# Layer norm tiles shared between VectorE and ScalarE, gate powers on GpSimd, residual and stores in pieces, and a new instruction order, in a small Flamingo decoder on one core

## The reference

```
for layer in 0..3:
    x = x + tanh(g_xattn[layer]) * attention_layer(layernorm(x), ctx)     # stages 0, 2, 4, 6
    x = x + tanh(g_ffn[layer])   * ffn_layer(layernorm(x))                # stages 1, 3, 5, 7
layernorm(x) = (x - mean(x)) / sqrt(var(x) + 1e-5)        # over the 128 columns
```

## Time and profile before

| | us |
|---|---|
| Median of 3 runs (316.25 to 316.88) | 316.64 |
| Profiled execution | 317.1 |
| Its span, first to last instruction | 315.3 |
| PE busy in the span | 296.9 |
| DVE busy | 231.4 |
| ACT busy | 149.2 |
| POOL busy | 63.7 |

### The profile page before, as it was taken

One profiled execution on the slowest core, in us unless ns is written; L12 is line 12 of the kernel. 1 busy time (PEld: TensorE's weight loads), 2 busy tenths in 40 slices (PEclk: granted clock), 3 DMA queues, 4 the chain that ended last, 5 costly groups with the idle time before them and its releaser, 6 DMA issues.

```text
span 315.3 us, 5757 instructions
## 1 busy us (share of the span) xinstructions
PE 296.9 (94%) x2088; PEld 199.5 (63%) x2088; DVE 231.4 (73%) x670; ACT 149.2 (47%) x330; POOL 63.7 (20%) x95
## 2 busy tenths in 40 slices
PE   8899999998899999999999999999999997998963
PEld 3463453793436488888888365589788774666431
DVE  4882985789768389796796495465558569999995
ACT  0448255422555864542306637523426538876411
POOL 5242454334100001000303301010311502211020
PEclk9999999999999999999999999999999999999999
DMA  6970300002200000000000000000000000000002
GB/s 185 309 248 0 102 13 3 0 2 75 73 0 2 0 2 0 3 0 2 0 0 2 3 1 2 0 2 0 0 2 0 2 1 0 3 0 0 3 0 67
DMA packets 8976, 8.73 MB, mean 28 GB/s; under 512 B 3547, under 2 KB 6901, under 8 KB 8949
## 3 DMA queue, kind: packets, MB, share of 16 engines
q1 hardware_dynamic: 8949, 8.37, 8.7%
HBM read 7.84 MB, written 0.52 MB: 27 GB/s over the span
## 4 chain that ended last, share of the span: by engine, by line
PE 65%; DVE 21%; ACT 6%; issue 3%; POOL 2%; DMA 2%; DVEq 0%; SPq 0%; ACTq 0%
PE psum L996 59%; DVE wide L1901 3%; DVE mx L1734 3%; ACT wide L1396 3%; PE psum L1090 2%; DMA early<-in_ffn 2%; DVE xn_t L1919 1%; DVE xn L1921 1%; DVE q L1914 1%; DVE wide L1908 1%; DVE wide L1907 1%; PE psum L1128 1%; DVE nmax L1868 1%; PE psum L1176 1%; PE psum L1184 1%
## 5 line engine op out<-in xcount | busy, mean ns | idle before, releaser
L934 POOL TENSOR_TENSOR nw<-mv,minus_half 128x2 f32<-128x2 f32 x32 | 22.2, 708 | 143.5 <-DVE mv L1597 143.5
L1396 ACT ACTIVATE wide<-psum 128x512 f32<-128x512 f32 x72 | 37.0, 607 | 14.9 <-PE psum L996 14.7
L1734 DVE TENSOR_REDUCE mx<-psum 128x4 f32<-128x308 f32 x96 | 38.6, 471 | 6.0 <-PE psum L996 5.9
L1396 ACT ACTIVATE q<-psum 128x512 f32<-128x512 f32 (+1 forms) x30 | 17.8, 597 | 36.0 <-PE psum L996 28.1
L996 PE MATMUL psum<-q_hi,first_hi 128*128 128x512 f32 (+1 forms) x68 | 30.6, 450 | 0.0
L996 PE MATMUL psum<-wide 78*128 78x386 f32 (+1 forms) x69 | 25.5, 507 | 3.0 <-DVE wide L1885 1.9
L996 PE MATMUL psum<-q_lo,first_hi 128*128 128x512 f32 (+1 forms) x68 | 26.8, 394 | 0.0
L996 PE MATMUL psum<-q_hi,first_lo 128*128 128x512 f32 (+1 forms) x68 | 26.7, 393 | 0.0
L996 PEld LDWEIGHTS psum<-early,wide 128*128 128x128 f32 x192 | 24.7, 191 | 2.3 <-ACT wide L1396 0.5
L996 PE MATMUL psum<-halves 128*128 128x512 bf16 x102 | 25.8, 379 | 0.0
L996 PE MATMUL psum<-early,wide 128*128 128x128 f32 x192 | 25.4, 276 | 0.1
(11 more groups left out here) (230 smaller groups left out, 562.8 us busy)
## 6 DMA issues: line engine op xcount, KB each, us to landing
early<-in_ffn SPq DMA_DIRECT2D x8, 256.0 KB, 4.8
w_attn<-in_attn SPq DMA_DIRECT2D x1, 640.0 KB, 7.4
w_attn<-in_attn SPq DMA_DIRECT2D x2, 288.0 KB, 6.4
x<-in_x SPq DMA_DIRECT2D x2, 256.0 KB, 3.6
w_ffn<-in_ffn SPq DMA_DIRECT2D x1, 512.0 KB, 7.2
early<-in_ffn SPq DMA_DIRECT2D x1, 512.0 KB, 3.7
out<-x SPq DMA_DIRECT2D x2, 256.0 KB, 2.3
rows<-in_rows SPq DMA_DIRECT2D x1, 468.0 KB, 6.1
```

Source lines behind the costliest of these rows:

```text
L934: G.tensor_tensor(nw[:, b, 2, tiles], mv[:, b, tiles, 1], minus_half[:, tiles], ALU.pow)\
L1396: A.activation(dst, banks.bank(*name)[0:rows_, 0:cols_], fn, **kw).then_inc(drained["act"], 1)
L1734: last = V.tensor_reduce(mx[:, b, t, lane_heads(g)], banks.bank("max", layer, b, t, g)[:, 0:GK].rearrange("p (h k) -> p h k", k=CTX), AX.X ...
```

## The change: what it does, and the diff

- **Norm.** For the pair h = 0, DVE only computes shift = -mean * rstd (one 128x2 instruction), and ACT, in a new step `scaled`, writes xn = rstd * x + shift for tiles 0 and 1 with two activations. DVE keeps tiles 2 and 3. `xn_ready` counts two tiles a stage, `scaled_ready` the other two; all who read xn wait for both.
- **gates1.** exp(gap) and exp(-logit) come from two powers on POOL with the bases e and 1/e; the sigmoid is 1 / (1 + exp(-logit)) with a reciprocal on DVE. ACT has no part in the gates now.
- **Residual of stage 6.** In the last GRU iteration x + gain * kept is computed in `gru_z`, and x - gain * nn in `gru_end` with a negated gain; slots are not formed and `slots_back` is gone. The norm of stage 7 waits for `slots_ready`.
- **quantised and stores.** The gain of stage 7 is folded into `rscale_b`. DVE scales two tiles, adds them, and signals; then the other two. SP stores each pair by itself, 128 KB.
- **Planner.** New costs for 14 kinds of steps, new dependences, and another LATER table for all three groups of steps, so a new order on every engine.

Left out of the diff: the LATER tables, semaphore and tile declarations, and the registration of steps.

```diff
         for h in range(2):
             step("norm", stage, h, ...
-                 then={"pool": in_order("pool", "norm", stage, h)}, dve=0.65, pool=0.72)
+                 then={"pool": in_order("pool", "norm", stage, h)}, dve=0.67, pool=0.72)
         for h in range(2):
-            step("norm_end", stage, h, after=[at("pool", "norm", stage, h)] + ..., dve=0.51)
+            step("norm_end", stage, h, after=[at("pool", "norm", stage, h)] + ...,
+                 dve=0.54 if h else 0.15)
+        step("scaled", stage, after=[at("dve", "norm_end", stage, 0)], act=0.85)
         if stage == 7:
-            step("integers", after=[at("dve", "norm_end", stage, 1)], dve=0.85)
-            step("rounded", after=[at("dve", "integers")], dve=0.65)
-            step("rounded_too", after=[at("dve", "integers")], act=0.6)
+            step("integers", after=[at("dve", "norm_end", stage, 1), at("act", "scaled", stage)], dve=0.99)
+            step("rounded", after=[at("dve", "integers")], dve=0.44)
+            step("rounded_too", after=[at("dve", "integers")], act=0.88)
...
-    step("gates1", after=[at("act", "turn", 3)], pe=0.92, dve=3.24, act=0.2)
-    step("weights_turn", after=[at("act", "gates1")], dve=1.97, pe=0.43, act=0.5)
+    step("gates1", after=[at("act", "turn", 3)], pe=0.92, dve=3.24, pool=1.4)
+    step("weights_turn", after=[at("pool", "gates1")], dve=2.2, pe=0.43, act=0.5)
...
-                 + in_order("dve", "gru_pair", it, i), dve=1.25)
+                 + in_order("dve", "gru_pair", it, i), dve=1.32)
...
         @block.sync
             for b in range(B):
-                sp.wait_ge(x_final[b], 1)
-                sp.dma_start(out[b].rearrange("(t p) d -> p t d", p=P), x[:, b, :, :]).then_inc(stored, 16)
-            sp.wait_ge(stored, 16 * B)
+                for h in range(T // 2):
+                    tiles = slice(2 * h, 2 * h + 2)
+                    sp.wait_ge(x_final[b], h + 1)
+                    sp.dma_start(out[b].rearrange("(t p) d -> p t d", p=P)[:, tiles, :], x[:, b, tiles, :])\
+                      .then_inc(stored, 16)
+            sp.wait_ge(stored, 16 * B * (T // 2))
...
         @block.gpsimd
+            def gates1(b):
+                pool.wait_ge(gap_ready[b], 1)
+                G.tensor_tensor(route_s[:, b, 4, :], e_powers[:, 0, :], route_s[:, b, 3, :], ALU.pow)
+                G.tensor_tensor(route_s[:, b, 7, :], e_powers[:, 1, :], lg[:, b, :, E1], ALU.pow).then_inc(second_ready[b], 1)
...
             def bias(b, stage):
-                pool.wait_ge(xn_ready[b], T * (stage + 1))
+                pool.wait_ge(xn_ready[b], 2 * stage + 2)
+                pool.wait_ge(scaled_ready[b], 2 * stage + 2)
...
         @block.tensor
             def turn(b, stage):
                     if stage == 7 and t >= T // 2:
                         pe.wait_ge(y_too_ready[b], t + 1 - T // 2)
+                    elif stage == 7 or t >= T // 2:
+                        pe.wait_ge(xn_ready[b], 2 * stage + t % 2 + 1)
                     else:
-                        pe.wait_ge(xn_ready[b], T * stage + t + 1)
+                        pe.wait_ge(scaled_ready[b], 2 * stage + t + 1)
...
         @block.scalar
             def out_bias(b):
+                A.activation(gain_neg[:, :], row("g"), ACT.Tanh, scale=-1.0)
                 A.activation(gain[:, :], row("g"), ACT.Tanh).then_inc(gain_ready, 1)
...
-                    empty(rscale_b[:, :], ACT.Copy, ("rscale",), cols_=D)
+                    act.wait_ge(gain_ready, 1)
+                    g = GAIN_OF[7]
+                    empty(rscale_b[:, :], ACT.Copy, ("rscale",), cols_=D, scale=gain[:, g:g + 1])
...
+            def scaled(b, stage):
+                act.wait_ge(shift_ready[b], stage + 1)
+                for t in pair(0):
+                    A.activation(xn[:, b, t, :], x[:, b, t, :], ACT.Identity, bias=shift[:, b, t:t + 1],
+                                 scale=nw[:, b, 2, t:t + 1]).then_inc(scaled_ready[b], 1)
...
-            def gates1(b):
-                act.wait_ge(gap_ready[b], 1)
-                A.activation(route_s[:, b, 4, :], route_s[:, b, 3, :], ACT.Exp)
-                A.activation(route_s[:, b, 7, :], lg[:, b, :, E1], ACT.Tanh, scale=0.5).then_inc(second_ready[b], 1)
...
         @block.vector
             def norm_end(b, stage, h):
                 dve.wait_ge(xn_rstd_ready[b], 2 * stage + h + 1)
-                for t in range(2 * h, 2 * h + 2):
+                if h == 0:
+                    V.scalar_tensor_tensor(shift[:, b, :], mv[:, b, 0:2, 0], -1.0, nw[:, b, 2, 0:2], ALU.mult, ALU.mult)\
+                     .then_inc(shift_ready[b], 1)
+                    return
+                for t in pair(1):
...
             def integers(b):
+                dve.wait_ge(scaled_ready[b], 2 * 7 + 2)
...
             def weights_turn(b):
-                link(V.tensor_scalar(shared_, shared_, 0.5, 0.5, ALU.mult, ALU.add))
+                link(V.tensor_scalar(shared_, shared_, 1.0, None, ALU.add))
+                link(V.reciprocal(shared_, shared_))
...
             def gru_z(b, it, h):
-                V.tensor_tensor(kept[:, b, tiles, :], tz[:, b, tiles, :], slots[:, b, tiles, :], ALU.mult)
+                last = V.tensor_tensor(kept[:, b, tiles, :], tz[:, b, tiles, :], slots[:, b, tiles, :], ALU.mult)
+                if it == ITERS - 1:
+                    link(last)
+                    g = GAIN_OF[6]
+                    V.scalar_tensor_tensor(flat(x[:, b, tiles, :]), flat(kept[:, b, tiles, :]), gain[:, g:g + 1],
+                                           flat(x[:, b, tiles, :]), ALU.mult, ALU.add)
...
             def gru_end(b, it, h):
+                if it < ITERS - 1:
+                    V.tensor_tensor(slots[:, b, tiles, :], kept[:, b, tiles, :], nn[:, b, tiles, :], ALU.subtract)\
+                     .then_inc(slots_ready[b], 1)
+                else:
+                    V.scalar_tensor_tensor(flat(x[:, b, tiles, :]), flat(nn[:, b, tiles, :]), gain_neg[:, g:g + 1],
+                                           flat(x[:, b, tiles, :]), ALU.mult, ALU.add).then_inc(slots_ready[b], 1)
...
             def quantised(b):
-                for t in range(T):
-                    last = V.scalar_tensor_tensor(xn[:, b, t, :], banks.bank("out", 7, b)[:, t * P:(t + 1) * P],
-                                                  route_s[:, b, 3, t:t + 1], rscale_b[:, :], ALU.mult, ALU.mult)
-                last.then_inc(drained["dve"], 1)
-                dve.wait_ge(*banks.emptied("out", 7, b))
-                V.scalar_tensor_tensor(flat(x[:, b, :, :]), flat(xn[:, b, :, :]), gain[:, g:g + 1],
-                                       flat(x[:, b, :, :]), ALU.mult, ALU.add).then_inc(x_final[b], 1)
+                for h in range(T // 2):
+                    tiles = slice(2 * h, 2 * h + 2)
+                    for t in pair(h):
+                        last = V.scalar_tensor_tensor(xn[:, b, t, :], banks.bank("out", 7, b)[:, t * P:(t + 1) * P],
+                                                      route_s[:, b, 3, t:t + 1], rscale_b[:, :], ALU.mult, ALU.mult)
+                    if h == 0:
+                        link(last)
+                    else:
+                        last.then_inc(drained["dve"], 1)
+                        dve.wait_ge(*banks.emptied("out", 7, b))
+                    V.tensor_tensor(x[:, b, tiles, :], x[:, b, tiles, :], xn[:, b, tiles, :], ALU.add)\
+                     .then_inc(x_final[b], 1)
```

More of the change, by code:

```diff
@@ L305, in bias @@
     def bias(stage):
-        step("bias", stage, after=[at("dve", "norm_end", stage, 1), prepared("dve", "out_bias")], pool=1.25)
+        step("bias", stage, after=[at("dve", "norm_end", stage, 1), at("act", "scaled", stage), prepared("dve", "out_bias")], pool=1.25)
     def down(phase, c, chunks, after):
@@ L375, in half_steps @@
     turn(5)
-    step("router", after=[at("act", "turn", 5)], pe=0.92, dve=1.74)
+    step("router", after=[at("act", "turn", 5)], pe=0.92, dve=1.82)
     step("choice_turn", after=[at("dve", "router")], pe=0.43, act=0.5, dve=0.33)
@@ L389, in half_steps @@
         for h in range(T // 2):
-            new = [at("dve", "gru_end", it - 1, h) if it else at("dve", "norm_end", 6, h)]
-            step("square", it, h, after=new + in_order("act", "square", it, h), act=0.56, pool=0.97)
-            step("slots_turn", it, h, after=new + in_order("act", "slots_turn", it, h), pe=0.24, act=0.32)
+            new = [at("dve", "gru_end", it - 1, h) if it else (at("dve", "norm_end", 6, 1) if h else at("act", "scaled", 6))]
+            step("square", it, h, after=new + in_order("act", "square", it, h), act=0.53, pool=0.97)
+            step("slots_turn", it, h, after=new + in_order("act", "slots_turn", it, h), pe=0.26, act=0.36)
         step("slot_products", it, after=[at("act", "slots_turn", it, 1), prepared("dve", "slots_in", 3)],
@@ L410, in half_steps @@
```

(12 more changed lines are left out.)

34 lines of the change are left out of this document (17 added, 17 removed), and 94 rows, old and new, of the table LATER.

## The result

The changed kernel takes 315.6 us (median; 315.3 to 315.92) where the kernel before, run beside it, takes 316.5 (316.2 to 317.1). The ratio is 0.9971, interval [0.9961, 0.9982]: 0.9 us or 0.3% faster. That is inside the range and on the forecast's side, but 0.9 us where 2.2 were forecast. Ratios are of undisturbed executions: one of the eleven of e7_query_first took 733.6 us and has no part in its ratio, though its median counts it (317.24; 317.1 without).

A forecast was written before the change was run, and what follows sets the result against it. PE was taken to bound 20 to 72 and 93 to 247 us, DVE 72 to 84 and 265 to 306, chains the rest. Work -0.9 and order -1.3 gave -2.2: 314.4 us against the median 316.64, range 311.5 to 317.7.

The forecast's parts named there:

- The three norms in DVE's stretches: Norm in 72 to 84 us and norm 7 of each half: -0.45, -0.45 and -0.3 us.
- the others behind the first `mx`: Norms where PE or a chain decides: DVE's saving is covered by PE's queue, taken as 0.
- the store: End of the kernel: last store carries half the bytes, -0.45 us (bounds 0 and -0.5).
- quantised: Tail: two pieces cost DVE more per half, +0.35 us (bounds 0.15 and 0.5).
- The first norm: Start: `scaled` on ACT near the first table load and `k_t`, +0.2 us.
- The residual: Last GRU pass: split operations each slightly longer on a full DVE, +0.2 us; one fewer after the last `n_ready`, 0.
- gates1: Between 93 and 247 us: activations and table loads leave ACT, powers go to POOL; covered by PE, 0.
- The cover that I named: 93 to 247 us: PE busy 153.65 of 154.00 us, so changes on other engines there count 0.
- the new order at -1.3: All engines' new order: middle between closing DVE's idle 4.6 us at 247 to 265 (-4.6) and more PE waits (+2).
- rival 3: New order closes DVE's gap after 247 us: 311.1 us, chance 0.09; against it, half 1's chain must run anyway.
- rival 1: `scaled` in ACT's queue delays evictions and holds PE up: 317.1 to 319.7 us, chance 0.16.
- The sum of my work terms: Norms, first norm, gates1, residual, quantised and stores together, without the order: -0.9 us.

The follow-up runs named there:

- e7_query_first: Changed kernel with one swap in ACT's order, query of half 1, layer 2, ahead of a block of half 0's score evictions: 317.24 us, ratio 1.0016.
- e3: Changed kernel with DVE scaling all four tiles of every norm again: 317.6 us, ratio 1.0025.
- e6: Kernel before with a tiny ACT copy ahead of its first wait, so that the table load comes early: 316.46 us, ratio 1.0.
- e4: Changed kernel with the last GRU pass's residual back in a piece of its own ahead of the norm: 316.05 us, ratio 0.9982.
- e10: Changed kernel with gates1 back on ACT, Exp and Tanh with their table loads: 316.28 us, ratio 1.0.
- e17: Changed kernel with the gates1 power that needs only lg made first: 315.51 us, ratio 0.996.
- e14: Changed kernel's new order with all old work: norm, residual, end and gates1 undone together: 318.68 us, ratio 1.0052.
- e8: Changed kernel with DVE's turn of half 1 put between the two pieces of half 0's quantised: 315.25 us, ratio 0.9959.
- e2: Kernel before's order and costs with all the new work, scaled and POOL's powers placed by its planned times: 320.4 us, ratio 1.012.
- e1: Changed kernel's new order with norm, residual and end as before, gates1 staying on POOL: 318.22 us, ratio 1.0052.

## Why the prediction was right and wrong

**Right: where each engine is the bound, and the norm.** The three norms in DVE's stretches were put at 0.45 + 0.45 + 0.3; undone (e3) they cost 0.46 up to the third `rinv` and 0.9 from the sixth `nmax` on, and the others behind the first `mx`, put at 0, cost 0.1 together. e3's busy time by stretch, 72 to 84 and 282 to 306, shows DVE full again:

```profile
72.00:84.00 12.00, 9.76 (x73) 4.91 (x76) 11.83 (x37) 3.49 (x8) 3.21 (x4) 1.00 0.34 96
282.00:306.00 24.00, 20.97 (x109) 11.96 (x110) 23.13 (x73) 10.02 (x27) 4.73 (x8) 1.00 0.00 1
```

**Right: the store**, 0.45 against 0.5, and quantised, 0.35 against 0.3.

**Small misses in the work.** The first norm, +0.2, stays open: e6 shows that its table load is covered, and its `scaled` wasn't tried alone. The residual, +0.2, is -0.33 (e4): the cost is there, 0.22 up to the sixth `nmax`, but I gave nothing to the 0.47 us taken from behind the last `n_ready`, and from there on the split gains 0.55 of body. gates1, 0, is -0.5 in the new order (e10): the powers are covered (e17), but the table loads they replace were not. The cover that I named, a PE busy for 153.65 of 154 us, hides such waits. Together, undone at once in the new order (e14), the work is worth 303.99 - 301.95 = 2.04 (2.6 by the ratios), where I had 0.9.

**The step that failed: the new order at -1.3.** With the old work the new order is worth +0.9 (bodies; +1.65 by the ratios). I took the middle between an idle gap of DVE (-4.6) and a quarter more waits of PE (+2), and it came out on the waits' side. The gap wasn't closed, as rival 3's own counterargument had it: 4.58 and 4.55 us. The waits came where PE sets the pace, and only there. PE's weight loads and matmuls between the third `rinv` and the last `back` wait for ACT and DVE, `issue` left out, 8.9 us in 19 waits before, 11.6 in 25 after and 12.1 in 27 in e14; the stretch itself takes 151.66, 152.60 and 153.07 us. The largest group, of before, after and e14 (columns as in the earlier trace rows):

```profile
PEld psum L996 <- ACT wide L1396: 2.4, 6, 0.6
```

```profile
PEld psum L1014 <- ACT wide L1416: 3.7, 6, 1.1
```

```profile
PEld psum L1009 <- ACT wide L1411: 3.7, 6, 1.1
```

Over the whole span these waits didn't grow (45.5, 43.3 and 44.5 us), and the group of the earlier trace rows went from 8.2 to 8.5: a sum over the span, which is what I priced the order by, hides what happens in the stretch that counts. e14 has no `scaled` on ACT and waits the same 3.7 us. So rival 1 had the place right, ACT's evictions that hold PE's loads, and the cause wrong: it is the order, not the norm's activations in ACT's queue. That it is these waits that cost the 0.9 is argued, not shown: they grow by 2.7 and 3.2 us where the stretch grows by 0.94 and 1.41. The sum of my work terms, -0.9, equals the result by chance: the parts were worth 2.0 and the order took 0.9 back (2.6 and 1.65 by the ratios).

The deeper fault is that "work, plus order" was a sum at all. The square above has a term of its own for the pair, 303.07 + 301.95 - 303.99 - 306.99 = -5.96 us (-6.4 by the ratios), larger than every other term; its size hangs in part on where I put the new steps in the old order. An order like this one is laid out for given durations, and work that changes them takes away what it had: that loss (3.9 here) and its recovery by a new order (5.0) are both larger than what the work itself saves (2.0).

**Left open.** Where in the tables the 0.9 us of the order come from beyond the stretches that the table of landmarks names, how often and why the granted clock falls in an execution's tail, and whether a better order for the new work exists. Only single places were tried, one for better (e8) and one for worse (e7).

## What to carry to other kernels

- When work moves between engines in a fixed order, the order is part of the price. Test the new order with the old work, and the old order with the new work, before crediting either.
- A stretch in which PE is busy from end to end can still hold waits. Look at its weight loads' waits before calling anything there covered, and say how much cover there is: 1.2 us for the powers here, and 2.0 more was too much.
- A body from one trace is one execution. Before reading a difference of half a microsecond out of two of them, compare their landmarks, their granted clock and their waits for loads: here 0.4 us came from a load and 0.65 from the clock.
- In a tail where one engine is full, every operation taken off it pays its length, if what it waits for is ready. Look for an idle 0.6 us there before looking anywhere else.

## What was unexpected of the hardware

- The first table load runs at 0.71 us in the changed kernel, ahead of the wait for `shift`, where before it ran at 7.18, behind the wait for PE. Both kernels wait and then activate. It goes with the first activation: at 0.71 where `scaled` comes first (e2 too), behind the wait where `k_t` does (5.94 in e3, 6.00 in e14, 7.44 in e1). Why wasn't tried.
- The start of one and the same program part varies by over a microsecond with the arrival of the first loads (first `mx` 11.46 to 12.89 us), more than the change is worth. A later load did the same once, by 0.4 us.
- PE's granted clock fell to half for 3.4 us in the tail of e1 and stayed full there in e14, with the same 2.74 us of idle PE ahead of it: 0.65 us, and as much as a whole term of the prediction.
- A power on POOL takes 0.71 us for 128x2 and 1.01 us for 128x4: not in proportion to the elements.
